# Two-layer attention in f32 on one core: a visit's two pair sums are folded into one before the product with ones

## The chip, the cores and the metric

The kernel runs on one core of a Trainium2 chip (trn2). The metric is device time in microseconds (us) of one execution, and the time before is the median of 3 runs. All arithmetic is in float32; a few operands are held as fp32r, a 32-bit format for products.

## The reference

`x` and `ctx` are [4, 1024, 512]. A softmax attention with 16 heads of 32 comes first, then a linear attention over the same context; both end in a layer norm.

```python
Q, K, V = heads(x @ Wq.T + bq), heads(ctx @ Wk.T + bk), heads(ctx @ Wv.T + bv)
att = softmax(Q @ K.T / sqrt(32))
x1 = layernorm((att @ V).merge() @ Wo.T + bo + x) * gamma0 + beta0
q_phi, k_phi = elu(x1), elu(ctx)
z = 1 / (q_phi @ k_phi.sum(axis=1) + 1e-6)
out = layernorm(x1 + (q_phi @ (k_phi.T @ ctx)) * z) * gamma1 + beta1
```

The softmax's denominator, the sum of the exponentials over the 1024 keys for each query and head, is what this change touches. It is the same sum after it, added in another order.

## The kernel before

The work of the first layer is cut into 64 units: 4 batches, 4 groups of four heads (QUAD), 4 chunks of 256 queries (CH). All five engines run the same counter `k` (a tick), from FIRST = -44 to LAST, and each writes its own instructions in the order of ticks; only semaphores hold them together. A unit takes 16 ticks. In tick `k`:

- TensorE (PE) does `pass1(k)` (L258): one product of 128 queries with 512 keys into one of three PSUM banks `score`, for the row maxima; VectorE (DVE) reduces it (`maximum`, L553). `pass1` waits until the maximum three uses back is taken.
- TensorE does `pass2(k-22)` (L282): the same scores turned, keys on partitions and queries along the row, into one of two banks `scoreT`; ScalarE (ACT) takes the exponential of a half step (`exponential`, L451) into `p_ring`, a ring of 8 key tiles of 4 x 256 columns.
- A planner, which is the same before and after, has spread "chains" over the ticks (`beside(k)`): the projections of K, V and Q, the output projection, the layer norms' tiles and the second layer.
- Once per unit, at tick 19 + 16u, `place_max(u)` (L267): the negated row maxima are turned by a product with the identity, and ScalarE copies them into rows 96 to 103 of `q_stack` (L441), from which `pass2` subtracts them. They come from VectorE, which at ticks 16, 17 and 18 (+16u) folds them (L563), rounds them (L570, a cast) and takes the rest of the rounding (L573, a tensor_tensor of `max_row` and `neg_max`). L573 is the instruction that `place_max` waits for (`max_split`).
- Every 8 ticks, at 35 + 8v, a visit `visit(v)`: 128 in all. TensorE first multiplies four key tiles of exponentials with V (L300) into `acc` columns 0 to 255, and then adds the denominators into `acc` columns 256 to 511 by products with a matrix of ones (L308). A product with ones sums over the 128 keys on the partitions, and its right-hand side is a sum of two key tiles that GpSimd (POOL) has added before (`add_pair`, L760: `pair_sum`, two slots, each written in two halves of 512 columns). Each f32 product of the program is two matrix instructions in the trace, so L300 has 32 of them per visit and L308 has 16, 8 for each of the two pairs.

Every other visit stands in the same tick as a `place_max` and right behind it: visit 2m at tick 35 + 16m behind `place_max(m+1)`. These ticks are called turns here; there are 63 of them and a first `place_max` without a visit.

GpSimd's `add_pair(pair, h)` stands at ticks 26 + 4·pair + h. Its first half waits until `divided` says that the products with ones have read the pair two before it, which lay in the same slot. So the first pair of visit v+1 waits for the first product of visit v. GpSimd also does the additions and scalings of the layer norms' tiles: L768 (bias), L773 and L776 (the root and the shift), L782 and L784, L789 and L791 (gamma and beta), and it adds features of the context (L803, L807).

VectorE's `normalise` (L582 to L597) divides `acc` by the denominators once a unit, after its second visit.

Of the kernel before, what the change touches and what calls it, by code (L numbers as in the profile page):

```python
# [7 lines left out]
ALU = mybir.AluOpType  # L8
# [4 lines left out]
def build(nc, x, xT, ctx, ctxT, WqT, bq, WkT, bk, WvT, bv, WoT, bo, gamma0, beta0, gamma1, beta1, out):  # L13
    B, S, D = x.shape
    P = nc.NUM_PARTITIONS
    DK = 32
    QUAD = P // DK
# [27 lines left out]
    FIRST = -44  # L45

# [4 lines left out]
    with ExitStack() as c:  # L51
# [6 lines left out]
        def sems(*names):  # L58
            return {n: c.enter_context(nc.semaphore(n)) for n in names}
# [66 lines left out]
                 "den_turned", "den_inverted", "den_back", "out_scaled", "f_phi", "ksum_kept", "y_summed",  # L126
# [3 lines left out]
        L = sems("cleared", "hot", "ident_made", "ones_made", "half_made", "paired", "totalled", "biased", "rooted0",  # L130
# [113 lines left out]
        def tensor_program():  # L244
# [42 lines left out]
            def visit(v):  # L287
# [16 lines left out]
                for s in range(VISIT // 2):  # L304
                    pair = VISIT // 2 * v + s
                    pe.wait_ge(L["paired"], 2 * (pair + 1))
                    for j in range(QUAD):
                        mm = pe.matmul(acc[j * DK:(j + 1) * DK, CH:2 * CH], ones[:, 0:DK],  # L308
                                       pair_sum[:, pair % 2, j * CH:(j + 1) * CH], start=False,
                                       stop=part == KT // VISIT - 1 and s == VISIT // 2 - 1,  # L310
                                       tile_position=(0, j * DK), skip_group_check=True)
                    mm.then_inc(T["divided"], 1)
# [231 lines left out]
        def vector_program():  # L544
# [31 lines left out]

            def normalise(unit, stage):
                if stage == 0:
                    dve.wait_ge(T["divided"], KT // 2 * (unit + 1))
# [132 lines left out]
            for k in range(FIRST, LAST):  # L712
# [32 lines left out]
                if k in phi_at:  # L745
                    make_phi(phi_at[k])
                unit, i = divmod(k - (VISIT_AT + 2 * VISIT + 1), UT)
# [4 lines left out]
        def gpsimd_program():  # L752
            pool = nc.gpsimd

            def add_pair(pair, h):
                n, cols = 2 * pair + 1, slice(h * HALF, (h + 1) * HALF)
                pool.wait_ge(A["exped"], 2 * n + h + 1)
                if h == 0 and pair >= 2:
                    pool.wait_ge(T["divided"], pair - 1)
                pool.tensor_tensor(pair_sum[:, pair % 2, cols], p_ring[:, (n - 1) % NP, cols], p_ring[:, n % NP, cols],  # L760
                                   ALU.add).then_inc(L["paired"], 1)
# [61 lines left out]
            for k in range(FIRST, LAST):  # L823
# [17 lines left out]
                if 0 <= pair < KT * UNITS // 2 and i < 2:  # L841
                    add_pair(pair, i)

# [170 lines left out]
```

## Time and profile before

| | before |
|---|---|
| median of 3 runs | 1755.48 us (1754.87 to 1761.07) |
| the profiled execution's own time | 1762.24 us |
| its span, first to last instruction | 1760.9 us |
| mean granted TensorE clock | 0.972 of 2.4 GHz |
| TensorE products busy | 1646.2 us (93%) |
| VectorE busy | 1070.9 us (61%) |
| GpSimd busy | 951.3 us (54%) |
| ScalarE busy | 880.9 us (50%) |

Busy times are sums over the whole span. Products of TensorE are pipelined and their ends are modelled, so how fast they follow each other is read from their starts. PEld is TensorE's weight load, which runs beside the products. In the timeline a row gives the start, the time to the last end of the merged instructions, the engine, the line, the operation with its operands and the count, and in brackets how long the engine had been idle and what ended that.

### The profile page before, as it was taken

The numbers are of one execution on the slowest core, as the hardware profiler recorded it, in microseconds if no ns is written. First come the engines' busy times: TensorE is split into PE (matmuls) and PEld (weight loads), VectorE is DVE, ScalarE is ACT, GpSimd is POOL, SyncE is SP. The second block draws the span as 40 slices with busy tenths as digits, with TensorE's granted clock in tenths as the row PEclk, the third lists the DMA queues.
The fourth block names the chain that finished last, engine by engine and source line by source line (L and its number), as shares of the span: only waits on it lengthen the run. The fifth ranks groups of instructions, "written<-read, shape, count | busy, mean of one in ns | idle before, by whom it ended". The sixth has DMA issues, their size and how long they took to land.

```text
span 1760.9 us, 32310 instructions
## 1 busy us (share of the span) xinstructions
PE 1646.2 (93%) x12176; PEld 1114.6 (63%) x12176; DVE 1070.9 (61%) x2216; ACT 880.9 (50%) x1617; POOL 951.3 (54%) x923
## 2 busy tenths in 40 slices
PE   6999999999999999999999999999999999999754
PEld 4667776676766666567666657657676767665321
DVE  2665557656666666567566756666666666666232
ACT  0355547555554554654554554665545554575321
POOL 0244535455655664455665655555566555566644
PEclk8999999999999999999999999999999999999877
DMA  8524162233315244141523234322322423200001
GB/s 252 159 63 132 55 204 78 73 99 103 108 40 138 79 130 162 55 115 39 144 79 110 74 103 146 110 85 91 112 72 91 122 74 102 97 24 13 25 24 36
DMA packets 149291, 168.05 MB, mean 95 GB/s; under 512 B 12816, under 2 KB 111120, under 8 KB 149136
## 3 DMA queue, kind: packets, MB, share of 16 engines
q1 hardware_dynamic: 149136, 165.99, 31.8%
q8 instruction: 97, 1.59, 0.4%
q14 instruction: 58, 0.48, 0.1%
HBM read 124.00 MB, written 41.94 MB: 94 GB/s over the span
## 4 chain that ended last, share of the span: by engine, by line
PE 81%; DVE 6%; POOL 4%; DMA 4%; issue 3%; ACT 2%; SPq 1%; DVEq 0%; ACTq 0%; POOLq 0%
PE acc L300 13%; PE score L258 13%; PE scoreT L282 12%; PE misc L375 6%; PE misc L329 6%; PE misc L367 6%; PE acc L308 6%; PE misc L339 6%; PE misc L351 5%; PE misc L319 4%; DVE maxes L553 2%; POOL pair_sum L760 1%; PE score L267 1%; DMA res_out<-ctx_nat 1%; DMA ctx_nat<-ctx_in 1%
## 5 line engine op out<-in xcount | busy, mean ns | idle before, releaser
L760 POOL TENSOR_TENSOR pair_sum<-p_ring 128x512 f32<-128x512 f32 x512 | 654.5, 1299 | 636.0 <-PE acc L308 568.5
L553 DVE TENSOR_REDUCE maxes<-score 128x1 f32<-128x512 f32 x1024 | 679.1, 678 | 441.6 <-PE score L258 440.5
L451 ACT ACTIVATE p_ring<-scoreT 128x512 f32<-128x512 f32 x1024 | 595.6, 594 | 616.8 <-PE scoreT L282 603.5
L258 PE MATMUL score<-k_stack,q_stack 96*128 96x512 f32 x1024 | 615.6, 603 | 8.7 <-DVE maxes L553 7.5
L282 PEld LDWEIGHTS scoreT<-q_stack,k_stack 104*128 104x128 f32 x2048 | 378.7, 191 | 187.8 <-ACT p_ring L451 114.4
L282 PE MATMUL scoreT<-q_stack,k_stack 104*128 104x256 f32 x2048 | 428.0, 291 | 16.3 <-ACT p_ring L451 14.8
L258 PEld LDWEIGHTS score<-k_stack,q_stack 96*128 96x128 f32 x1024 | 194.3, 190 | 170.4 <-issue 139.2
L300 PE MATMUL acc<-p_ring,v_sb 128*32 128x256 f32 x4096 | 279.4, 392 | 0.0
L300 PEld LDWEIGHTS acc<-p_ring,v_sb 128*32 128x32 f32 x4096 | 155.5, 112 | 81.6 <-ACT p_ring L451 22.2
L308 PE MATMUL acc<-pair_sum,ones 128*32 128x256 f32 x2048 | 159.3, 383 | 7.7 <-POOL pair_sum L760 7.7
L319 PE MATMUL misc<-xT_sb,wq 128*128 128x256 f32 x512 | 134.3, 386 | 10.1 <-DVE k_low L615 5.8
L329 PE MATMUL misc<-ctxT_sb,wk 128*128 128x512 f32 x256 | 133.2, 606 | 7.7 <-DMA ctxT_sb<-ctxT_in 6.9
L367 PE MATMUL misc<-kv_sb,ctx_nat 128*128 128x512 f32 x256 | 135.3, 623 | 4.5 <-issue 2.3
L339 PE MATMUL misc<-wv,ctxT_sb 128*128 128x128 f32 x1024 | 134.1, 275 | 0.0
L375 PE MATMUL misc<-ctx_nat,fphi_sb 128*128 128x512 f32 x256 | 132.1, 597 | 0.0
L351 PE MATMUL misc<-wo,outT 128*128 128x512 f32 x256 | 129.5, 597 | 0.0
L339 PEld LDWEIGHTS misc<-wv,ctxT_sb 128*128 128x128 f32 x1024 | 125.8, 192 | 0.6 <-DVE k_low L615 0.3
L308 PEld LDWEIGHTS acc<-pair_sum,ones 128*32 128x32 f32 x2048 | 87.2, 112 | 46.5 <-POOL pair_sum L760 10.0
L319 PEld LDWEIGHTS misc<-xT_sb,wq 128*128 128x128 f32 x512 | 90.2, 193 | 18.9 <-DVE k_low L615 6.0
L773 POOL TENSOR_TENSOR rstd<-var_eps,minus_half 128x1 f32<-128x1 f32 x64 | 36.5, 571 | 92.8 <-DVE var_eps L648 92.6
L441 ACT ACTIVATE q_stack<-score 8x1024 fp32r<-8x1024 f32 x64 | 65.0, 1016 | 41.5 <-PE score L267 41.0
L688 DVE SCALAR_TENSOR_TENSOR fphi_sb<-f_sb,ctx_nat 128x128 f32<-128x128 f32 x128 | 70.1, 547 | 22.6 <-ACT f_sb L506 11.0
(66 smaller groups left out, 1221.8 us busy)
## 6 DMA issues: line engine op xcount, KB each, us to landing
xT_sb<-xT_in SPq DMA_DIRECT2D x64, 512.0 KB, 4.1
k_stack<-k_dram SPq DMA_DIRECT2D x96, 256.0 KB, 4.4
q_stack<-q_dram SPq DMA_DIRECT2D x192, 128.0 KB, 2.5
ctxT_sb<-ctxT_in SPq DMA_DIRECT2D x8, 1024.0 KB, 7.3
k_dram<-k_high SPq DMA_DIRECT2D x32, 256.0 KB, 2.0
k_dram<-k_low SPq DMA_DIRECT2D x32, 256.0 KB, 2.6
q_dram<-q_high SPq DMA_DIRECT2D x64, 128.0 KB, 1.7
q_dram<-q_low SPq DMA_DIRECT2D x64, 128.0 KB, 1.9
```

Source lines behind the costliest of these rows:

```text
L258: pe.matmul(score[use % 3][:], q_stack[0:SPLIT, unit % NQ, j, t * P:(t + 1) * P], k_stack[0:SPLIT, unit // NC % 2 * QUAD + j, h * HALF:(h ...
L282: mm = pe.matmul(scoreT[k % 2][:, (j % 2) * CH:(j % 2 + 1) * CH], k_stack[0:ROWS, unit // NC % 2 * QUAD + j, kt * P:(kt + 1) * P], q_stack ...
L300: mm = pe.matmul(acc[j * DK:(j + 1) * DK, 0:CH], v_sb[:, group % 2, kt, j * DK:(j + 1) * DK], p_ring[:, n % NP, j * CH:(j + 1) * CH], star ...
L308: mm = pe.matmul(acc[j * DK:(j + 1) * DK, CH:2 * CH], ones[:, 0:DK], pair_sum[:, pair % 2, j * CH:(j + 1) * CH], start=False, stop=part == ...
L319: mm = pe.matmul(bank_of("Q", unit)[:, 0:CH], wq[:, t, :], xT_sb[:, unit % 2, t, :], start=t == 0, stop=t == G - 1)
L329: mm = pe.matmul(bank_of("K", i)[:], wk[:, t, :], ctxT_sb[:, h, t, :], start=t == 0, stop=t == G - 1)
L339: mm = pe.matmul(bank_of("V", i)[:, t * P:(t + 1) * P], ctxT_sb[:, h, f, t * P:(t + 1) * P], wv[:, f, :], start=f == 0, stop=f == G - 1)
L367: mm = pe.matmul(bank_of("A", tile)[:], phiT_sb[:, d * P:(d + 1) * P], kv_sb[:, d, :], start=d == 0, stop=d == G - 1)
L375: pe.matmul(bank_of("S", i)[:], fphi_sb[:, piece % NPHI, :], ctx_nat[:, t, :], start=t == 0, stop=t == KT - 1).then_inc(T["kv_piece"], 1)
L451: act.activation(p_ring[:, n % NP, h * HALF:(h + 1) * HALF], scoreT[k % 2][:], ACT.Exp, scale=SCALE).then_inc(A["exped"], 1)
L553: dve.reduce_max(maxes[:, unit % 2, t, j, h:h + 1], score[bank_use[k] % 3][:], AX.X).then_inc(V["maxed"], 1)
L760: pool.tensor_tensor(pair_sum[:, pair % 2, cols], p_ring[:, (n - 1) % NP, cols], p_ring[:, n % NP, cols], ALU.add).then_inc(L["paired"], 1)
```

## The change

The second pair's sum of a visit is added onto the first pair's before TensorE reads it: GpSimd adds columns 0 to 511 (`add_quad` in its program), VectorE columns 512 to 1023 (`add_quad` in its program). A visit then has one product with ones (8 matrix instructions) instead of two. The slots of `pair_sum` are dealt anew by `place_of_pair`: pairs 0, 1, 2, 3 lie in slots 0, 1, 1, 0, so the first pair of the next visit lies where the second pair of this one lay, and waits for both `add_quad` of this visit instead of for TensorE. The second pair of a visit waits for the visit before.

```diff
@@
+    def place_of_pair(pair):
+
+        return (pair // 2 + pair % 2) % 2
@@
-                for s in range(VISIT // 2):
-                    pair = VISIT // 2 * v + s
-                    pe.wait_ge(L["paired"], 2 * (pair + 1))
-                    for j in range(QUAD):
-                        mm = pe.matmul(acc[j * DK:(j + 1) * DK, CH:2 * CH], ones[:, 0:DK],
-                                       pair_sum[:, pair % 2, j * CH:(j + 1) * CH], start=False,
-                                       stop=part == KT // VISIT - 1 and s == VISIT // 2 - 1,
-                                       tile_position=(0, j * DK), skip_group_check=True)
-                    mm.then_inc(T["divided"], 1)
+                pe.wait_ge(L["quad_low"], v + 1)
+                pe.wait_ge(V["quad_high"], v + 1)
+                for j in range(QUAD):
+                    mm = pe.matmul(acc[j * DK:(j + 1) * DK, CH:2 * CH], ones[:, 0:DK],
+                                   pair_sum[:, place_of_pair(2 * v), j * CH:(j + 1) * CH], start=False,
+                                   stop=part == KT // VISIT - 1, tile_position=(0, j * DK), skip_group_check=True)
+                mm.then_inc(T["divided"], 1)
@@ vector_program
+            def add_quad(v):
+
+                first, second = (pair_sum[:, place_of_pair(2 * v + i), HALF:2 * HALF] for i in range(2))
+                dve.wait_ge(L["paired"], 4 * (v + 1))
+                dve.tensor_tensor(first, first, second, ALU.add).then_inc(V["quad_high"], 1)
+
             def normalise(unit, stage):
                 if stage == 0:
-                    dve.wait_ge(T["divided"], KT // 2 * (unit + 1))
+                    dve.wait_ge(T["divided"], KT // VISIT * (unit + 1))
@@
                 if k in phi_at:
                     make_phi(phi_at[k])
+                v, i = divmod(k - VISIT_AT + 2, 2 * VISIT)
+                if i == 0 and 0 <= v < VISITS:
+                    add_quad(v)
                 unit, i = divmod(k - (VISIT_AT + 2 * VISIT + 1), UT)
@@ gpsimd_program
                 pool.wait_ge(A["exped"], 2 * n + h + 1)
-                if h == 0 and pair >= 2:
-                    pool.wait_ge(T["divided"], pair - 1)
-                pool.tensor_tensor(pair_sum[:, pair % 2, cols], p_ring[:, (n - 1) % NP, cols], p_ring[:, n % NP, cols],
-                                   ALU.add).then_inc(L["paired"], 1)
+                if h == 0 and pair >= 2 and pair % 2:
+                    pool.wait_ge(T["divided"], pair // 2)
+                elif h == 0 and pair >= 2:
+                    pool.wait_ge(L["quad_low"], pair // 2)
+                    pool.wait_ge(V["quad_high"], pair // 2)
+                pool.tensor_tensor(pair_sum[:, place_of_pair(pair), cols], p_ring[:, (n - 1) % NP, cols],
+                                   p_ring[:, n % NP, cols], ALU.add).then_inc(L["paired"], 1)
+
+            def add_quad(v):
+
+                first, second = (pair_sum[:, place_of_pair(2 * v + i), 0:HALF] for i in range(2))
+                pool.wait_ge(L["paired"], 4 * v + 3)
+                pool.tensor_tensor(first, first, second, ALU.add).then_inc(L["quad_low"], 1)
@@
                     add_pair(pair, i)
+                if 0 <= pair < KT * UNITS // 2 and pair % 2 and i == 2:
+                    add_quad(pair // 2)
```

Three places of the engines' orders show it. The first is VectorE around a turn, in an early unit; the names in brackets are the semaphores waited for. Before, from the cast of the maxima (L570) to the next division of `acc` (L582):

```order
L570 CAST neg_max<-max_row 128x2x4 [waits max_turned,max_whole]
L553 TENSOR_REDUCE maxes<-score 128x1 [waits scored]
L573 TENSOR_TENSOR neg_max<-max_row,neg_max 128x2x4 [waits max_high]
L553 TENSOR_REDUCE maxes<-score 128x1 [waits scored] x10
L582 STREAM_TRANSPOSE den_rows<-acc 128x256 [waits out_scaled,divided]
```

And the same place now (the kernel's lines have moved, L570 is L572, L573 is L575, L553 is L555, L582 is L590):

```order
L572 CAST neg_max<-max_row 128x2x4 [waits max_turned,max_whole]
L583 TENSOR_TENSOR pair_sum<-pair_sum 128x512 [waits paired]
L555 TENSOR_REDUCE maxes<-score 128x1 [waits scored]
L575 TENSOR_TENSOR neg_max<-max_row,neg_max 128x2x4 [waits max_high]
L555 TENSOR_REDUCE maxes<-score 128x1 [waits scored] x7
L583 TENSOR_TENSOR pair_sum<-pair_sum 128x512 [waits paired]
L555 TENSOR_REDUCE maxes<-score 128x1 [waits scored] x3
L590 STREAM_TRANSPOSE den_rows<-acc 128x256 [waits out_scaled,divided]
```

One of a unit's two new additions (L583) stands between the cast and the subtraction of the maxima, the other seven maxima behind it.

The second place is GpSimd in the same early units, over one visit. Before:

```order
L760 TENSOR_TENSOR pair_sum<-p_ring 128x512 [waits divided,exped]
L760 TENSOR_TENSOR pair_sum<-p_ring 128x512 [waits exped]
L760 TENSOR_TENSOR pair_sum<-p_ring 128x512 [waits divided,exped]
L760 TENSOR_TENSOR pair_sum<-p_ring 128x512 [waits exped]
L760 TENSOR_TENSOR pair_sum<-p_ring 128x512 [waits divided,exped]
```

Now:

```order
L774 TENSOR_TENSOR pair_sum<-p_ring 128x512 [waits quad_high,quad_low,exped]
L774 TENSOR_TENSOR pair_sum<-p_ring 128x512 [waits exped]
L774 TENSOR_TENSOR pair_sum<-p_ring 128x512 [waits divided,exped]
L774 TENSOR_TENSOR pair_sum<-p_ring 128x512 [waits exped]
L781 TENSOR_TENSOR pair_sum<-pair_sum 128x512 [waits paired]
L774 TENSOR_TENSOR pair_sum<-p_ring 128x512 [waits quad_high,quad_low,exped]
```

A fifth addition (L781) follows a visit's four, and the next visit's first one waits for VectorE's half instead of for TensorE.

The third place is TensorE at a visit. Before:

```order
L282 MATMUL scoreT<-q_stack,k_stack 128x256 x2
L300 MATMUL acc<-p_ring,v_sb 32x256 x16
L308 MATMUL acc<-pair_sum,ones 32x256 x8
L258 MATMUL score<-k_stack,q_stack 128x512
L282 MATMUL scoreT<-q_stack,k_stack 128x256 x2
```

Now:

```order
L286 MATMUL scoreT<-q_stack,k_stack 128x256 x2
L304 MATMUL acc<-p_ring,v_sb 32x256 x16
L311 MATMUL acc<-pair_sum,ones 32x256 x4
L262 MATMUL score<-k_stack,q_stack 128x512
L286 MATMUL scoreT<-q_stack,k_stack 128x256 x2
```

Four products with ones (8 matrix instructions in the trace) are gone; nothing else has moved.

## Rows read from the trace of the kernel before

**Rows 1.** The page: busy time, share and instructions; then the granted clock.

```profile
PE 1646.2 (93%) x12176; PEld 1114.6 (63%) x12176; DVE 1070.9 (61%) x2216; ACT 880.9 (50%) x1617; POOL 951.3 (54%) x923
...
PEclk8999999999999999999999999999999999999877
```

**Rows 2.** Groups by line: busy us, mean ns of one | idle before, releaser.

```profile
L760 POOL TENSOR_TENSOR pair_sum<-p_ring 128x512 f32<-128x512 f32 x512 | 654.5, 1299 | 636.0 <-PE acc L308 568.5
...
L300 PE MATMUL acc<-p_ring,v_sb 128*32 128x256 f32 x4096 | 279.4, 392 | 0.0
...
L308 PE MATMUL acc<-pair_sum,ones 128*32 128x256 f32 x2048 | 159.3, 383 | 7.7 <-POOL pair_sum L760 7.7
```

**Rows 3.** Waits: us in total, times, longest us.

```profile
POOL pair_sum L760 <- PE acc L308: 568.5, 126, 9.2
...
PEld score L267 <- DVE neg_max L573: 32.1, 38, 1.6
...
PEld acc L308 <- POOL pair_sum L760: 10.0, 6, 6.4
...
PE score L267 <- DVE neg_max L573: 15.8, 20, 1.4
...
PE score L258 <- DVE maxes L553: 7.5, 20, 0.9
```

**Rows 4.** Timeline of TensorE, visit 3, which is no turn.

```profile
109.66 1.93 PE L300 MATMUL acc<-p_ring,v_sb 128*32 128x256 f32 x32
...
111.42 1.05 PE L308 MATMUL acc<-pair_sum,ones 128*32 128x256 f32 x16
...
112.39 0.50 PE L258 MATMUL score<-k_stack,q_stack 96*128 96x512 f32 x1
```

**Rows 5.** Timeline, VectorE and TensorE at the turn of unit 2.

```profile
100.86 0.16 DVE L570 CAST neg_max<-max_row 128x8 fp32r<-128x8 f32 x1
100.93 0.68 DVE L553 TENSOR_REDUCE maxes<-score 128x1 f32<-128x512 f32 x1
...
101.53 0.15 DVE L573 TENSOR_TENSOR neg_max<-max_row,neg_max 128x8 fp32r<-128x8 f32 x1
...
101.74 0.28 PE L267 MATMUL score<-ident,neg_max 128*8 128x128 f32 x1 [0.69 <-DVE neg_max L573]
...
105.41 4.88 DVE L553 TENSOR_REDUCE maxes<-score 128x1 f32<-128x512 f32 x8 [3.12 <-PE score L258]
```

**Rows 6.** Timeline of GpSimd, the four additions ahead of that turn.

```profile
93.94 4.99 POOL L760 TENSOR_TENSOR pair_sum<-p_ring 128x512 f32<-128x512 f32 x4 [5.64 <-PE acc L308]
```

**Rows 7.** Timeline at the turn of unit 19, with GpSimd busy.

```profile
498.61 0.34 DVE L570 CAST neg_max<-max_row 128x8 fp32r<-128x8 f32 x1
498.87 0.68 DVE L553 TENSOR_REDUCE maxes<-score 128x1 f32<-128x512 f32 x1
498.89 1.26 POOL L782 TENSOR_TENSOR ctx_nat<-ctx_nat,gamma_row 128x512 f32<-128x512 f32 x1
499.47 0.70 DVE L573 TENSOR_TENSOR neg_max<-max_row,neg_max 128x8 fp32r<-128x8 f32 x1
...
500.22 0.28 PE L267 MATMUL score<-ident,neg_max 128*8 128x128 f32 x1 [1.39 <-DVE neg_max L573]
```

**Rows 8.** One line's instructions: duration ns, min/median/max.

```profile
L573 DVE TENSOR_TENSOR neg_max<-max_row,neg_max x64: 149/156/1190, 60.2 to 1621.5; 128x8 fp32r<-128x8 f32 x64
...
L656 DVE SCALAR_TENSOR_TENSOR ctx_nat<-ctx_nat x32: 682/1124/1741, 393.0 to 1743.5; 128x512 f32<-128x512 f32 x32
```

**Rows 9.** Timeline at the turns of units 12 and 13: subtraction done, turn begun.

```profile
325.38 0.15 DVE L573 TENSOR_TENSOR neg_max<-max_row,neg_max 128x8 fp32r<-128x8 f32 x1
...
325.97 0.28 PE L267 MATMUL score<-ident,neg_max 128*8 128x128 f32 x1
...
352.01 0.16 DVE L573 TENSOR_TENSOR neg_max<-max_row,neg_max 128x8 fp32r<-128x8 f32 x1
...
353.78 0.28 PE L267 MATMUL score<-ident,neg_max 128*8 128x128 f32 x1
```

**Rows 10.** The chain that ended last, its piece around the last visits.

```profile
1636.90 2.51 POOL pair_sum L760 x2
1639.42 1.23 POOL ctx_nat L789
...
1661.08 1.23 POOL pair_sum L760
1662.35 1.08 PE acc L308 x8
```

More of the change, by code:

```diff
@@ L125, in build @@
         V = sems("hot_rows", "k_low_kept", "q_low_kept", "v_kept", "maxed", "max_whole", "max_high", "max_split",
-                 "den_turned", "den_inverted", "den_back", "out_scaled", "f_phi", "ksum_kept", "y_summed",
+                 "quad_high", "den_turned", "den_inverted", "den_back", "out_scaled", "f_phi", "ksum_kept", "y_summed",
                  "counted0", "aggregated0", "var_added0", "phi_made", "dotted", "z_added", "z_inverted",
                  "y_attended", "counted1", "aggregated1", "var_added1", "bias_spread", "bias_folded")
-        L = sems("cleared", "hot", "ident_made", "ones_made", "half_made", "paired", "totalled", "biased", "rooted0",
+        L = sems("cleared", "hot", "ident_made", "ones_made", "half_made", "paired", "quad_low", "totalled", "biased", "rooted0",
                  "shifted0", "scaled0", "x1", "rooted1", "shifted1", "scaled1", "result")
```

## The prediction

> **What bounds the kernel now.** I read the page first. TensorE's products are busy 93% of the span, no other engine more than 61%, and the granted clock is at its upper level, 2.4 GHz, in nearly every slice until the last [rows 1]. The waits come next: of the many thousand products very few wait for anybody. VectorE's maxima hold `pass1` up for 7.5 us in all, and the largest wait inside the steady part is `place_max` for the subtraction L573: 20 times TensorE itself stood idle, 15.8 us in all, and 38 times the weight load did [rows 3]. So whatever shortens TensorE's own work shortens the run, and whatever comes late at `place_max` lengthens it. GpSimd waits 568.5 us for TensorE's products with ones [rows 3]; it has time, but it is held up.
>
> **What goes away.** 128 visits lose 8 of 16 instructions of L308. Two prices can be read. By the group's busy time half of 159.3 us goes, 79.6 us [rows 2]. But these are modelled ends that overlap. By the starts, the 32 instructions of L300 hand over to L308 after 111.42 - 109.66 = 1.76 us, 55 ns each; and L308's 16 hand over to `pass1` after 112.39 - 111.42 = 0.97 us [rows 4]. 16 x 55 ns are 0.88 us, the rest (0.1 us) is the run-out at the end, which stays. I take 8 x 55 ns = 0.44 us per visit, x 128 = **-56 us**, and keep 79.6 for the range.
>
> **What is added on GpSimd.** 128 additions of 128x512, 1.30 us each [rows 2], 166 us. GpSimd is free for that: 951 us of 1761 busy, and it loses most of the 568.5 us in which it waits for TensorE, because a visit's first pair no longer waits for the products with ones. Cost on the path: 0, as long as `quad_low` comes before TensorE ends the V products of the visit. At the turn of unit 2 GpSimd's four pair additions end at 93.94 + 4.99 = 98.93 [rows 6], the fifth would end at 100.2, and TensorE asks for it 1.76 us after the turn's start at 101.74 [rows 4, 5], at 103.5. Where GpSimd is late by a layer norm's two additions (2.6 us) that margin is just used up; its earlier start of the first pair gives these back.
>
> **What is added on VectorE.** 128 additions of 128x512 with both inputs in SBUF. The trace has no such addition. The nearest is L656, as wide and with two inputs in SBUF, 682 ns at the shortest [rows 8]; eight maxima in a row, 680 ns each by their own rows, take 4.88 us, 0.61 us from start to start [rows 5]. So an addition puts 0.61 us into VectorE's row and its result is there after 0.69. The Trainium skill, VectorE: DVE Perf Modes, section The TRN2 errata, gives (N+151)/0.96 ns for such an addition, 691 ns, which agrees with L656; its section The DRAIN you can't avoid says that the next instruction does not start before the pipeline is empty. By that rule it would cost the full 0.69, some 4 us more over the run; the maxima show 0.61 and I stay with them.
>
> Half of these, 64, stand behind nothing urgent: the addition before visits 1, 3, 5 and so on (no turns) is followed by two maxima, and TensorE then spends 2.7 us on the visit, in which VectorE sits idle (3.12 us at a turn [rows 5]). They cost 0, and if that cover were gone, 0.6 us each, 38 us.
>
> The other 63 are the point. They stand between the cast L570 and the maximum ahead of L573, and L573 releases TensorE at the turn. First the 0.61 us. Then a second thing. When VectorE's half is done, GpSimd is released for the next visit's first pair, whose exponentials are long there, and starts at once. L573 reads two operands in SBUF, and such instructions do not run while GpSimd adds: alone it takes 156 ns [rows 8]; at unit 19 GpSimd began an addition at 498.89, L573 began at 499.47 and ended at 500.17, 20 ns behind GpSimd's end at 500.15 [rows 7]. TensorE started 0.05 us later, and its wait was 1.39 instead of the 0.69 us of a quiet turn [rows 5, 7].
>
> So, from the cast's end: before, the maximum starts at 0, L573 at 0.60, is done at 0.75, TensorE starts at 0.80 [rows 5]. After: the addition starts at 0, the maximum at 0.61, the addition is done at 0.69, GpSimd runs from 0.74 to 2.01, L573 could start at 1.21 but ends at 2.04, TensorE starts at 2.09. A turn is **1.3 us later**, more than what its own visit and the next one save together (0.88).
>
> Whether TensorE feels it depends on the slack of the turn. In 20 turns it was already idle (15.8 us [rows 3]): full 1.3 each, 26 us. In the other 18 of the 38 where only the load queue waited, the slack is like unit 12's: L573 done at 325.53, turn begun at 325.97, 0.4 us of slack [rows 9], so 0.9 each, 16 us. In the remaining 26 (25 turns and the first `place_max`) the slack is longer, up to unit 13's 1.6 us [rows 9]; between 0.6 and 0 each I take 0.3, 8 us. Together **+50 us**. Bounds: without the lock-out by GpSimd 20 x 0.6 + 18 x 0.2 = 16 us; with no slack anywhere 63 x 1.3 = 82 us.
>
> **The tail.** Around the last two visits the chain runs over GpSimd and DMA [rows 10]. The first pair of visit 126 no longer waits for visit 125 (2.5 us at 1636.90), and two fifth additions come in (2 x 1.3). I take 0, within 3 us either way.
>
> **Sum.** 1762.24 - 56 + 50 = 1756.2 us against the profiled execution's own time, 6 us less. That execution lies 6.8 us above the median of 1755.48, so against the median the forecast is **1750 us**: the products saved are handed back at the turns.
>
> **Rival A, the turns cost little.** L573 slips in before GpSimd starts, or TensorE has more slack there than I read: then the turns cost 16 us, and the time is 1755.5 - 56 + 16 = 1716. For it: GpSimd could be at another instruction, or the second half of that pair's exponentials could hold it. Against it: L573's 0.70 in [rows 7], and its longest of 1190 ns [rows 8]. The Trainium skill, SBUF — State Buffer, section SBUF: two separate sides, calls the port pair an exclusive lock that the first comer keeps for its whole instruction; by that the rival would need GpSimd idle, and the trace agrees. 0.13.
>
> **Rival B, the products with ones are dearer than their pitch.** The saving is the 79.6 us of the busy time, and the time is 1755.5 - 79.6 + 50 = 1726. Against it stands the regular pitch in [rows 4]. 0.10.
>
> **Rival C, VectorE waits for GpSimd at the turns: slower.** VectorE's addition needs GpSimd's pair, and in the moment the pair is ready GpSimd begins its own fifth addition and shuts VectorE's out for 1.28 us. It decides where the pair ends less than 1.3 us before the cast is done. At unit 2 the distance is 101.02 - 98.93 = 2.1 us [rows 5, 6], a margin of 0.8; at unit 19 the cast itself was held until 498.95 by an addition [rows 7], so there the margin is gone. If it is gone at the 38 turns with little slack, at 0 to 1.28 us and 0.64 on the mean, that adds 24 us: 1774. Against it: GpSimd starts the pairs earlier than before. 0.17.
>
> **That it doesn't do what it says** is excluded by the order of the instructions: 4 products with ones per visit instead of 8, five GpSimd additions instead of four.
>
> **How the numbers follow.** A difference of 0.5%, 8.8 us, is about what a measurement of this kernel can tell from none: faster means below 1746.7, slower above 1764.3. My forecast's own range is 1738 to 1764 (turns between 38 and 64 us), chance 0.55, of which 0.20 lies below 1746.7. Rivals A and B, 0.23, are all faster. Rival C, 0.17, is slower but for 0.02; small things in its direction (a visit that waits for `quad_low`) or mine make 0.05 more within 0.5%. Faster 0.43, same 0.42, slower 0.15. The range takes in nearly all of A and C: 1718 to 1776.
>
> **What would show it.** The wait of `place_max` for VectorE's subtraction grows from 15.8 us to some 60 us, in 50 turns or more instead of 20; the subtraction's median goes from 156 ns to about 0.8 us, ending with a GpSimd addition; L308's successor has half its count and 0.53 us from its start to the next `pass1`; GpSimd's wait for TensorE, 568.5 us, nearly vanishes; `pass1`'s wait for the maxima stays below 20 us. The forecast is wrong if the subtraction stays at 156 ns (rival A), if the visit shrinks by 0.6 us or more (B), or if VectorE's new addition itself has a mean far above 0.7 us at the turns (C).

## The result, and the profile after

The changed kernel is slower: 1783.3 us at the median of 4 runs (1782.0 to 1784.8) against 1757.0 of the kernel before beside it, ratio 1.0147 (95% interval 1.0125 to 1.0169). The forecast was 1750 us, range 1718 to 1776: the time lies outside it. The profiled execution took 1781.96 us, 19.7 more than the one of before (1762.24).

The page of the changed kernel, busy times and granted clock, beside [rows 1]:

```profile
PE 1610.7 (90%) x11152; PEld 1100.2 (62%) x11152; DVE 1212.2 (68%) x2344; ACT 883.0 (50%) x1617; POOL 1134.8 (64%) x1051
...
PEclk9999999999999999999999999999999999898877
```

TensorE has 1024 matrix instructions less and is busy 35.5 us less, and the run is longer all the same. The list of waits of the changed kernel (us in total, times, longest), which answers to [rows 3]:

```profile
POOL pair_sum L774 <- DVE pair_sum L583: 146.9, 66, 5.3
...
PE score L271 <- DVE neg_max L575: 66.5, 53, 2.7
...
PEld acc L311 <- POOL pair_sum L781: 25.3, 8, 10.9
...
PE acc L311 <- DVE pair_sum L583: 11.2, 7, 3.7
...
PE score L262 <- DVE maxes L555: 7.3, 21, 0.9
```

`place_max` (now L271) waits 66.5 us for the subtraction instead of 15.8, in 53 turns instead of 20. GpSimd's wait for TensorE is gone. The subtraction itself, by its own line (ns, min/median/max), beside the 156 ns of [rows 8]:

```profile
L575 DVE TENSOR_TENSOR neg_max<-max_row,neg_max x64: 153/934/1220, 58.4 to 1637.2; 128x8 fp32r<-128x8 f32 x64
```

And one turn in the timeline, that of unit 2, the same as in [rows 5]:

```profile
99.49 0.16 DVE L572 CAST neg_max<-max_row 128x8 fp32r<-128x8 f32 x1
99.56 0.69 DVE L583 TENSOR_TENSOR pair_sum<-pair_sum 128x512 f32<-128x512 f32 x1
100.16 0.69 DVE L555 TENSOR_REDUCE maxes<-score 128x1 f32<-128x512 f32 x1
100.42 2.50 POOL L774 TENSOR_TENSOR pair_sum<-p_ring 128x512 f32<-128x512 f32 x2 [2.45 <-ACT p_ring L453]
100.76 0.94 DVE L575 TENSOR_TENSOR neg_max<-max_row,neg_max 128x8 fp32r<-128x8 f32 x1
...
101.76 0.39 PE L271 MATMUL score<-ident,neg_max 128*8 128x128 f32 x2 [2.06 <-DVE neg_max L575]
```

The addition takes 0.60 us from its start to the next, GpSimd is released and starts at 100.42 (0.17 us behind the addition's end at 100.25; I had put it at 0.05), and the subtraction ends at 101.70, when GpSimd's first half (1.28 us) does. From the cast's end at 99.65 to TensorE's start are 2.11 us; before they were 101.74 - 101.02 = 0.72. A turn without slack waits 2.06 us instead of 0.69.

The visit is shorter as forecast: at visit 3, which is no turn, the products with ones and what follows are

```profile
110.99 0.61 PE L311 MATMUL acc<-pair_sum,ones 128*32 128x256 f32 x8
111.53 0.50 PE L262 MATMUL score<-k_stack,q_stack 96*128 96x512 f32 x1
```

0.54 us apart, where [rows 4] have 0.97. Summed over 127 visits, from the start of the products with ones to the next start behind them, it is 95.0 us instead of 150.6: 55.6 us saved.

So the two terms of my sum are right to a microsecond each (-55.6 against -56, and the 50.7 us by which the waits of `place_max` grew against +50), and what makes the time wrong is something else. The granted clock in stretches of 100 us shows most of it (columns: stretch, length, busy us and instructions of PE, PEld, DVE, ACT, POOL, then the granted clock, DMA share, GB/s). Before:

```profile
100.00:200.00 100.00, 95.69 (x852) 70.91 (x852) 60.50 (x122) 52.18 (x89) 49.02 (x40) 1.00 0.33 95
...
1100.00:1200.00 100.00, 97.52 (x698) 62.02 (x698) 64.75 (x130) 61.80 (x142) 54.47 (x64) 1.00 0.34 103
```

After:

```profile
100.00:200.00 100.00, 90.80 (x752) 66.58 (x753) 68.84 (x122) 49.12 (x85) 58.34 (x47) 0.97 0.31 92
...
1100.00:1200.00 100.00, 93.75 (x608) 58.77 (x599) 73.89 (x133) 59.45 (x137) 64.03 (x71) 0.95 0.29 88
```

A stretch of 100 us with a granted clock of 0.95 has spent 10 us at 1.2 GHz and the rest at 2.4 GHz. Over the steady part, from 60 us to visit 122, the records of the granted clock add up to 20.5 us at 1.2 GHz before and 61.4 us after; over the whole span the mean fell from 0.972 to 0.959, and it is 0.956 to 0.959 in all four runs. What the lower clock costs is seen at a turn at 1121 us:

```profile
1121.84 0.38 PE L271 MATMUL score<-ident,neg_max 128*8 128x128 f32 x1 [2.06 <-DVE neg_max L575]
1121.95 0.65 PE L304 MATMUL acc<-p_ring,v_sb 128*32 128x256 f32 x3
...
1125.34 0.67 PE L311 MATMUL acc<-pair_sum,ones 128*32 128x256 f32 x3
```

TensorE stands idle 2.06 us, and the visit behind it runs its products with V in 3.4 us (1121.95 to 1125.34) instead of 1.75. The falls lie at such waits: of the 15 in the steady part of the changed kernel 9 begin within 1 us of the end of a wait of 2.0 to 2.7 us at a turn. Such a wait does not always bring a fall: 17 turns wait longer than 2 us.

The balance of the 19.7 us, read from the starts of all visits. Up to visit 122, products with ones -51.6, waits at the turns +48.8 (the last 1.7 of the 50.5 lie behind it), the time from a visit's first product with V to its first with ones +19.7 (14 of it in visits at 1.2 GHz, 6 in visits 45, 77 and 109, which wait for VectorE's half), and everything else -3.4; together visit 122 starts 13.5 us later. Over the whole run the waits of `pass2` for ScalarE alone are 9.6 us shorter (5.2 instead of 14.8). Visit 45 shows how a half comes late: GpSimd finishes the second pair only at 620.66, and then its own fifth addition holds VectorE's, which takes 1.74 us instead of the median 0.68.

```profile
619.38 1.28 POOL L774 TENSOR_TENSOR pair_sum<-p_ring 128x512 f32<-128x512 f32 x1
620.63 1.26 POOL L781 TENSOR_TENSOR pair_sum<-pair_sum 128x512 f32<-128x512 f32 x1
620.70 1.74 DVE L583 TENSOR_TENSOR pair_sum<-pair_sum 128x512 f32<-128x512 f32 x1 [2.32 <-POOL pair_sum L774]
```

Behind visit 122 come 6.3 us more. They are TensorE's waits at the products with ones of visits 126 and 127: 14.1 us (3.7 and 10.4) instead of 7.7, and behind the last of them both kernels take 98 us more. In visit 127 GpSimd finishes the second pair at 1677.8 and starts its fifth addition only at 1680.63, because two instructions of a layer norm (L802 and L804, gamma and beta) stand between them in its order:

```profile
1676.52 1.26 POOL L774 TENSOR_TENSOR pair_sum<-p_ring 128x512 f32<-128x512 f32 x1
1677.73 1.26 POOL L802 TENSOR_TENSOR ctx_nat<-ctx_nat,gamma_row 128x512 f32<-128x512 f32 x1
1679.08 1.59 POOL L804 TENSOR_TENSOR ctx_nat<-ctx_nat,beta_row 128x512 f32<-128x512 f32 x1
1680.63 1.26 POOL L781 TENSOR_TENSOR pair_sum<-pair_sum 128x512 f32<-128x512 f32 x1
```

### The profile page after: what moved, and what is told of

The parts are those of the page before. It is cut to its first block, busy times and chain, and to the rows that moved or that the text cites. A ratio compares the mean times of both kernels' runs of the same rounds, so it can differ in the third digit from the quotient of the medians.

```text
span 1780.6 us, 30646 instructions
## 1 busy us (share of the span) xinstructions
PE 1610.7 (90%) x11152; PEld 1100.2 (62%) x11152; DVE 1212.2 (68%) x2344; ACT 883.0 (50%) x1617; POOL 1134.8 (64%) x1051
## 4 chain that ended last, share of the span: by engine, by line
PE 71%; DVE 15%; POOL 5%; issue 4%; DMA 3%; ACT 2%; SPq 0%; DVEq 0%; ACTq 0%; POOLq 0%
PE acc L304 14%; PE score L262 11%; PE scoreT L286 10%; PE misc L369 6%; PE misc L377 6%; PE misc L341 5%; PE misc L331 5%; DVE maxes L555 5%; PE misc L321 4%; PE acc L311 4%; PE misc L353 4%; DVE neg_max L575 2%; DVE pair_sum L583 2%; POOL pair_sum L774 1%; PE score L271 1%
## 5 line engine op out<-in xcount | busy, mean ns | idle before, releaser
L555 DVE TENSOR_REDUCE maxes<-score 128x1 f32<-128x512 f32 x1024 | 680.9, 678 | 320.7 <-PE score L262 320.1
L304 PE MATMUL acc<-p_ring,v_sb 128*32 128x256 f32 x4096 | 289.8, 405 | 0.0
L304 PEld LDWEIGHTS acc<-p_ring,v_sb 128*32 128x32 f32 x4096 | 171.2, 116 | 74.3 <-ACT p_ring L453 22.6
L781 POOL TENSOR_TENSOR pair_sum<-pair_sum 128x512 f32<-128x512 f32 x128 | 166.5, 1301 | 0.0
L793 POOL TENSOR_TENSOR rstd<-var_eps,minus_half 128x1 f32<-128x1 f32 x64 | 41.9, 655 | 143.9 <-DVE var_eps L656 143.9
L583 DVE TENSOR_TENSOR pair_sum<-pair_sum 128x512 f32<-128x512 f32 x128 | 109.9, 859 | 31.5 <-POOL pair_sum L774 31.5
L311 PE MATMUL acc<-pair_sum,ones 128*32 128x256 f32 x1024 | 104.9, 393 | 21.6 <-DVE pair_sum L583 11.2
L271 PE MATMUL score<-ident,neg_max 128*8 128x128 f32 x256 | 43.3, 298 | 66.5 <-DVE neg_max L575 66.5
```

Of the source, the lines that this page charges most:

```text
L304: mm = pe.matmul(acc[j * DK:(j + 1) * DK, 0:CH], v_sb[:, group % 2, kt, j * DK:(j + 1) * DK], p_ring[:, n % NP, j * CH:(j + 1) * CH], star ...
L555: dve.reduce_max(maxes[:, unit % 2, t, j, h:h + 1], score[bank_use[k] % 3][:], AX.X).then_inc(V["maxed"], 1)
```

## The experiments

The runs e1 to e4 tell the parts apart, e5 to e8 test the cause of the lower clock and cheap remedies, e9 to e11 move `place_max` itself. Ratios are to runs of the kernel before on the same chip beside them, whose median was 1762.2 us for e1 to e4, 1759.3 for e5 to e8 and 1758.8 for e9 to e11. The columns: TensorE's own wait in `place_max`; time at 1.2 GHz between 60 us and visit 122; start of visit 122.

| kernel | ratio (95% interval) | wait at turns, us | 1.2 GHz, us | visit 122 at, us |
|---|---|---|---|---|
| before | 1 | 16 | 20 | 1599 |
| changed | 1.0147 (1.0125 to 1.0169) | 66 | 61 | 1613 |
| e1_tick34 | 0.9798 (0.9778 to 0.9818) | 20 | 27 | 1559 |
| e2_pool_held | 0.9967 (0.9950 to 0.9983) | 42 | 58 | 1587 |
| e3_no_quads | 0.9776 (0.9756 to 0.9795) | 31 | 44 | 1564 |
| e4_two_products | 1.0438 (1.0418 to 1.0457) | 66 | 72 | 1669 |
| e5_turns_late | 0.9792 (0.9765 to 0.9818) | 20 | 31 | 1557 |
| e6_stall_alone | 1.0251 (1.0228 to 1.0274) | 44 | 61 | 1640 |
| e7_addition_alone | 1.0182 (1.0159 to 1.0205) | 36 | 51 | 1628 |
| e8_last_two | 0.9793 (0.9766 to 0.9819) | 20 | 34 | 1555 |
| e9_place_inside | 0.9801 (0.9777 to 0.9825) | 7 | 34 | 1558 |
| e10_late_and_inside | 0.9755 (0.9732 to 0.9778) | 1 | 17 | 1548 |
| e11_before_inside | 0.9939 (0.9918 to 0.9961) | 0 | 17 | 1587 |

### e1_tick34: VectorE's addition behind the subtraction

```diff
-                v, i = divmod(k - VISIT_AT + 2, 2 * VISIT)
+                v, i = divmod(k - VISIT_AT + 1, 2 * VISIT)
                 if i == 0 and 0 <= v < VISITS:
                     add_quad(v)
```

> The changed kernel with VectorE's new addition one tick later in its order, behind the subtraction of the maxima (tick 34 + 8v instead of 33 + 8v); all else as changed. The turn theory (the addition and the GpSimd addition that it releases stand before the subtraction that place_max waits for, and the 10 more windows of half clock in the changed kernel are a consequence of those stalls): the subtraction's median goes back to about 0.16 us, place_max waits under 18 us instead of 66.5, the half-clock windows in the steady part go back to 7 or so, and the time is about 1757 - 56 + 5 (tail) + 5 (visits that wait for a half) = 1711 us. The load theory (the clock falls because VectorE and GpSimd do more at the same time as TensorE, wherever the addition stands): the stalls go but the extra half clock stays, some 18 us: 1729 us. The late-halves rival (the visit's own waits for the two additions cost as much as the turns did): 1750 us or more, with VectorE's addition waited for at the products with ones.

Measured: ratio 0.9798, 1721 us on the scale of 1757. The subtraction's line and the waits at the turns in this kernel:

```profile
L575 DVE TENSOR_TENSOR neg_max<-max_row,neg_max x64: 149/156/1190, 59.1 to 1580.7; 128x8 fp32r<-128x8 f32 x64
...
  PE score L271: 19.0, 20
```

One place in VectorE's order is worth 3.5% of the time. The change as it was made loses 1.5%, the same change with the addition 0.7 us later wins 2.0%. The turn theory holds (the waits are 19.0 us, a little over the 18 forecast), the late-halves rival falls, and so does the load theory: the load is the same and the time at 1.2 GHz is down from 61 to 27 us. Of the 10 us over the forecast of 1711 some 7 are the visits' own waits for the two halves: 11.8 us up to visit 122, where I had put 5 (over the whole run 16.7 us in 15 visits for VectorE's half and 8.6 for GpSimd's).

### e2_pool_held: GpSimd released only behind the subtraction

```diff
                     pool.wait_ge(V["quad_high"], pair // 2)
+                    if pair % 4 == 2 and pair < 228:
+                        pool.wait_ge(V["max_split"], (pair - 2) // 4 + 2)
```

> The changed kernel, but GpSimd holds the next visit's first pair addition at 57 of the 63 turns until the subtraction of the maxima is done, so only VectorE's own addition stays ahead of the subtraction. If the turn's 1.3 us is made of 0.6 (VectorE's addition) and 0.7 (the lock-out by GpSimd's pair addition): the subtraction's median falls from 0.93 to 0.16 us, place_max's wait falls from 66.5 to about 30 us, and the time from 1783 to about 1747 or, with fewer half-clock windows, 1740. If the lock-out is not what holds the subtraction: the median stays near 0.9 and the time within 5 us of 1783.

Measured: ratio 0.9967; the waits are 41.4 us in 36 turns, the median 157 ns:

```profile
L575 DVE TENSOR_TENSOR neg_max<-max_row,neg_max x64: 147/157/1037, 59.8 to 1611.6; 128x8 fp32r<-128x8 f32 x64
```

The lock-out is what held the subtraction. Of the 50.7 us more at the turns 25 belong to GpSimd's released addition, and 22 to VectorE's own (from here to e1_tick34). The waits that are left are somewhat more than forecast, 41 against 30 us; six of the turns weren't held. The span is 26 us shorter than the changed kernel's. On the scale of 1757 the time is 1751, where I had forecast 1747, or 1740 with a recovered clock: the clock did not recover, with 58 us at 1.2 GHz against 61. So 24 us less of stalls gave 26 us back here, and the time at 1.2 GHz does not go in proportion to the stalls.

### e3_no_quads: the product alone

Neither addition is made; the second pair of each visit is left out of the denominators.

```diff
-                pe.wait_ge(L["quad_low"], v + 1)
-                pe.wait_ge(V["quad_high"], v + 1)
+                pe.wait_ge(L["paired"], 4 * (v + 1))
...
                 elif h == 0 and pair >= 2:
-                    pool.wait_ge(L["quad_low"], pair // 2)
-                    pool.wait_ge(V["quad_high"], pair // 2)
+                    pool.wait_ge(L["paired"], 2 * pair)
```

> The changed kernel without both new additions: the product with ones reads the first pair's sum alone, and the second pair is left out of the denominators. It still waits for both pairs, and GpSimd's pairs are in the new slots. It measures what the product that is gone is worth by itself. By the pitch of the instructions (0.44 us a visit): 1757 - 56 = 1701 us, 1695 to 1708 with the few waits at turns that are left. By the modelled busy time (79.6 us): 1678. If the clock fell because TensorE issues fewer products (and not because of stalls), the extra half-clock windows are here too and the time is near 1718.

Measured: 0.9776, 1718 on the scale of 1757, not 1701. The products with ones are shorter by the full 53 us, and 15 us of it are lost at the turns (31 instead of 16 us) with 44 us at 1.2 GHz. The cause is in the slots: a visit's first pair no longer waits for TensorE, so GpSimd adds close to the turn, with no new addition anywhere. Here it is the cast ahead of the subtraction that is held: its median is 725 ns instead of 160, the subtraction's stays at 157. At the turn of unit 2 GpSimd adds from 96.16 to 98.65, and the cast ends 0.03 us behind it:

```profile
96.16 2.49 POOL L769 TENSOR_TENSOR pair_sum<-p_ring 128x512 f32<-128x512 f32 x2 [1.37 <-ACT p_ring L452]
...
97.57 1.11 DVE L571 CAST neg_max<-max_row 128x8 fp32r<-128x8 f32 x1
```

The forecast for this run named 1718 for a clock that falls with the number of products. The number came true, and the mechanism is another: e6_stall_alone has all the products and the lower clock, e10_late_and_inside has the fewer products and 17 us at 1.2 GHz. So the number can't stand for that theory.

### e4_two_products: the additions alone

TensorE issues the product with ones twice from the same sum, so the denominators come out doubled.

```diff
-                for j in range(QUAD):
-                    mm = pe.matmul(acc[j * DK:(j + 1) * DK, CH:2 * CH], ones[:, 0:DK],
...
+                for s in range(2):
+                    for j in range(QUAD):
+                        mm = pe.matmul(acc[j * DK:(j + 1) * DK, CH:2 * CH], ones[:, 0:DK],
...
```

> The changed kernel with the product with ones issued twice from the same sum (denominators doubled): the additions and their waits as changed, TensorE's work as before. It measures the additions' cost alone. If gain and cost add up, 1783 + 56 = 1839 us, place_max's wait again 60 to 70 us, and again 15 or more half-clock windows in the steady part. If the shorter visit was part of the cause of the stalls or of the lower clock (VectorE and GpSimd have less time to catch up), the time stays below 1825 and place_max waits for less.

Measured: 1.0438; the profiled span is 1837.7 us, 57.1 more than the changed kernel's. The two ratios put it at 51 us, uncertain by some 5, since the changed kernel and this one were measured beside different runs of the kernel before. `place_max` waits 66.0 us, as in the changed kernel. Gain and cost add up: the shorter visit had no part in the stalls.

### e5_turns_late and e8_last_two: two refinements

```diff
-                v, i = divmod(k - VISIT_AT + 2, 2 * VISIT)
-                if i == 0 and 0 <= v < VISITS:
-                    add_quad(v)
+                for late in range(2):
+                    v, i = divmod(k - VISIT_AT + 2 - late, 2 * VISIT)
+                    if i == 0 and 0 <= v < VISITS and (v % 2 == 0) == bool(late):
+                        add_quad(v)
```

> The changed kernel with VectorE's new addition behind the subtraction of the maxima at the turns (tick 34, as in the run e1_tick34, ratio 0.980), but left at tick 33 + 8v at the other visits, where nothing waits for the subtraction. In e1_tick34 8 of those other visits waited 0.45 us for it, and visits 45, 51, 77, 83 and 109 about 2 us. If the later place caused the short waits, they go (3.6 us) and perhaps two of the long ones: ratio 0.976 to 0.979. If placement at the other visits does not matter, 0.980.

Measured: 0.9792 against 0.9798, within the intervals. The short waits for VectorE's half went (15 waits of 16.7 us became 7 of 13.5), the long ones stayed.

In e8_last_two VectorE also makes GpSimd's half of visits 126 and 127:

```diff
+                if v >= VISITS - 2:
+                    lows = [pair_sum[:, place_of_pair(2 * v + i), 0:HALF] for i in range(2)]
+                    dve.tensor_tensor(lows[0], lows[0], lows[1], ALU.add).then_inc(V["quad_last"], 1)
```

> The run e5_turns_late with GpSimd's half of the last two visits given to VectorE too. In the changed kernel GpSimd's fifth additions stand in the chain of the last visits (1663.0 and 1680.7 us), and the stretch from visit 122 to the end took 167.9 instead of 161.6 us. If the fifth additions lengthen it, it becomes 2 to 3 us shorter than in e5_turns_late; if the tail's length is set by the layer norms' loads and stores alone, it stays within 1 us.

Measured: the stretch from visit 122 to the end is 163.3 us against 164.0, the ratio 0.9793. Within 1 us, but this edit moves the work and does not take it away: in visits 126 and 127 TensorE now waits 10.9 us for VectorE where it waited 12.4. So it does not clear the additions. e3_no_quads, which has neither, takes 159.9 us for this stretch with 8.3 us of such waits, against 163.3 to 169.1 us in the eight kernels with both additions and 161.6 in the kernel before.

### e6_stall_alone: a stall and no work

```diff
                 pe.wait_ge(V["max_split"], unit + 1)
+                pe.wait_ge(V["maxed"], min(PLACE + UT * unit + 1, HALVES))
```

> The kernel before with one added wait and no added work: at each turn place_max also waits until VectorE has taken the maximum of its own tick. TensorE then stands still some 0.3 to 0.6 us longer at most turns, and no engine does anything more. If stalls at the turns are what brings the half-clock windows: place_max's waits grow from 16 to 40 to 50 us, the windows between 60 us and visit 122 from 20 us to 45 or more, and the time grows by the stalls plus some 10 us, to a ratio of 1.02 to 1.03. If the additional work of VectorE and GpSimd brings them: the windows stay at 20 us or so and the ratio is 1.015 to 1.02, by the stalls alone.

Measured: 1.0251. Every engine has the kernel before's work. TensorE stands 27.7 us longer at the turns (44 against 16), and visit 122 starts 41.0 us later. Three stretches of this kernel, for the clock:

```profile
100.00:200.00 100.00, 93.44 (x819) 68.31 (x821) 56.63 (x113) 49.37 (x84) 44.90 (x36) 0.97 0.32 93
400.00:500.00 100.00, 95.05 (x702) 66.88 (x700) 63.54 (x136) 50.12 (x85) 55.68 (x51) 0.98 0.31 93
1100.00:1200.00 100.00, 96.46 (x709) 63.47 (x708) 63.18 (x129) 56.42 (x122) 49.36 (x55) 0.97 0.32 101
```

The time at 1.2 GHz rises from 20 to 61 us, as in the changed kernel, and all four runs have a mean clock of 0.960 or 0.961 where the seven runs of before beside them have 0.967 to 0.975. So stalls at the turns cost more than their own length here: 13 us on top of 28. The visits show where: from first product with V to first with ones they take 14.7 us more in all.

### e7_addition_alone: VectorE's addition, waited for by nobody

The kernel before, with one addition more into a new buffer `scratch`.

```diff
+                v, i = divmod(k - VISIT_AT + 2, 2 * VISIT)
+                if i == 0 and 0 <= v < VISITS:
+                    dve.wait_ge(M["rows"], 5 * 16)
+                    if v > 0:
+                        dve.wait_ge(V["added"], v)
+                    dve.tensor_tensor(scratch[:], gamma0_row[:], beta0_row[:], ALU.add).then_inc(V["added"], 1)
```

> The kernel before with a 128x512 addition of two constant rows into a buffer that nobody reads, at the place in VectorE's order where the change has its own; nothing waits for it and GpSimd is not released by it. The turn theory says 0.6 us of the 1.3 us belong to this addition: place_max's waits 16 us to about 35 us (20 turns by 0.6, 18 by 0.2, plus lock-outs by chance), the subtraction's median stays 0.16, ratio 1.01 to 1.02, half-clock windows somewhat above 20 us. If the whole cost of a turn came from the addition and none from the released GpSimd work, place_max's waits would be near 66 us and the ratio 1.04.

Measured: 1.0182, waits 35.6 us in 32 turns. The addition's own part is 20 us of stalls, as the split of 0.6 and 0.7 says, and 9 more came with them (visit 122 starts 29 us later, with 51 us at 1.2 GHz).

### e9, e10, e11: the turned maxima inside the visit

TensorE does `place_max` between the visit's products with V and its product with ones. In the changed kernel (e9_place_inside), with the additions of e5_turns_late (e10_late_and_inside) and in the kernel before (e11_before_inside):

```diff
                 mm.then_inc(T["weighted"], 1)
+                if v % 2 == 0 and v // 2 + 1 < UNITS:
+                    place_max(v // 2 + 1)
...
-                if i == 0 and 0 <= unit < UNITS:
+                if i == 0 and unit == 0:
                     place_max(unit)
```

> The changed kernel with VectorE's and GpSimd's orders untouched; only TensorE does place_max between the visit's products with V and its product with ones instead of ahead of the visit. The 1.3 us by which the subtraction is late then lies beside 1.75 us of products with V. If the turn was all that made the changed kernel slow: place_max's waits fall from 66.5 us to a few, the half-clock windows before visit 122 from 61 us to 20 or 30, and the ratio to before becomes 0.970 to 0.980. If ScalarE's copy of the turned maxima (1.0 us, now 1.8 us later) becomes the next wait, part comes back as waits of pass2 for ScalarE: 0.98 to 0.99.

> Both remedies: VectorE's addition behind the subtraction at the turns (e5_turns_late, ratio 0.979) and place_max between the products with V and with ones. The 19.6 us of waits left at the turns should go and some half clock with them: ratio 0.963 to 0.970. If the subtraction is no longer urgent, this kernel and e9_place_inside differ by less than 0.003, since it no longer matters where VectorE's addition stands.

> The kernel before with place_max between the visit's products with V and with ones, nothing else. It had 16 us of waits there, and some half clock: 1757 - 16 - 5 = 1736, ratio 0.988. Against e9_place_inside it gives what the change is worth where no turn is in its way: 56 us of products less some 6 us of waits at visits and in the tail, that is a ratio between the two of 0.970 to 0.975. If ScalarE's later copy costs TensorE a wait, the ratio is 0.995 or above.

Measured: 0.9801, 0.9755 and 0.9939. e9 leaves VectorE and GpSimd as in the changed kernel, the subtraction's median is still 0.95 us, and the kernel goes from 1.5% slower to 2.0% faster, since the 1.75 us of products with V now lie over it. TensorE's waits for ScalarE in `pass2` rose from 5.2 us in the changed kernel to 17.4. Waits of TensorE in e10_late_and_inside:

```profile
PE acc L313 <- DVE pair_sum L585: 17.4, 10, 3.8
PE scoreT L286 <- ACT p_ring L455: 15.4, 18, 2.3
PE acc L313 <- POOL pair_sum L784: 11.9, 4, 8.6
```

`place_max`'s wait is down to 1.4 us and the time at 1.2 GHz to 17 us. But 10 us of new waits for ScalarE came in (15.4 us; in e5_turns_late 5.0): its copy of the turned maxima now comes later, before the first `pass2` that needs it. The waits at the products with ones are 7 us longer too (29.3 us against 22.2). These two fit the distance from the forecast of 0.963 to 0.970; no run takes them apart. e9 and e10 differ by 0.005, more than the 0.003 I allowed: e9 still has waits of 7 us at its turns, and twice the time at 1.2 GHz. e10_late_and_inside beats both kernels, 1713.5 us against 1758.8.

e11 came out at 0.9939 where I had forecast 0.988: the 16 us of waits at the turns are gone, and TensorE's waits for ScalarE in `pass2` rose from 14.8 to 23.2 us. Against e11, the same order without the change, the change is worth 0.985 in e9 and 0.981 in e10, the latter some 33 us of the 56 that it takes from TensorE. I had expected 0.970 to 0.975.

## Why the prediction was wrong

- **What goes away**, -56 us: right. 55.6 us by the starts of the visits, and 57.1 between the profiled spans of the changed kernel and e4_two_products. Rival B (79.6 us by busy times) is refuted: ends of overlapping products are no price, starts are.
- **GpSimd's additions cost 0 in the steady part**: nearly right; it is waited for in 8 visits by the weight loads, 1.2 to 2.2 us each in six of them, and the long ones (4.1 and 10.9 us) lie in the tail.
- **VectorE's addition, 0.61 us into its row**: right, 0.60 in the timeline. In the prediction I took the Trainium skill, VectorE: DVE Perf Modes, section The DRAIN you can't avoid, to ask for the full 0.69. That was half of what it states: the same paragraph says that a next operation that is not held starts earlier. The row agrees with that, the next maximum starts 0.60 us behind the addition's start.
- **The turn, 1.3 us and +50 us in all**: right, 1.37 us at a turn without slack and +50.7 us. The 20 turns that waited before gave 24 of it (forecast 26), the others 26.5 (forecast 24). The split of 0.6 for the addition and 0.7 for GpSimd's lock-out fits e2, e7 and e1. A slip on the way did no harm: from the cast's end to TensorE's start the rows give 0.72 us and not 0.80, because I counted from the start of the next instruction, before and after alike.
- **The additions before the other visits cost 0**: off by the 6 us of visits 45, 77 and 109, where GpSimd's layer-norm additions delay the visit's second pair, VectorE's addition waits for it, and GpSimd's fifth addition then holds it up.
- **The sum** is the step that failed. It left the granted clock at its level of [rows 1] and took a stall of TensorE to cost its own length. The stalls at the turns brought TensorE down to 1.2 GHz for three times as long, 61 us instead of 20 up to visit 122, which cost some 14 us in the visits' products with V; e6_stall_alone shows the same with stalls alone, 13 us on top of 28. In e2_pool_held the stalls fell by 24 us and the time at 1.2 GHz by only 3, so no price per microsecond of stall can be read from these runs. With the 6 us of the late halves, 6 us in the tail and some 3 us gained elsewhere this makes up the 19.7 us of the profiled executions.
- **The tail**, taken as 0 within 3 us: off by 6.3 us. TensorE waits 14.1 us for the additions of the last two visits instead of 7.7, and without the additions (e3_no_quads) the stretch is no longer than before.
- **The conversion to the median** was wrong too: I took off 6.8 us because one profiled execution of before lay that far above the median. Later medians of the kernel before were 1757 to 1762 us, so this was scatter of the runs, and the changed kernel's profiled execution lay 1.3 us below its median. Some 7 of the 33 us between 1750 and 1783 are this, the other 26 are the distance between the -6 us forecast for the profiled execution and its +19.7.
- **Rival A** fell with the subtraction's median of 934 ns.
- **Rival C** had the right sign and almost the right time (1774) and the wrong mechanism: VectorE's addition took more than 0.8 us at only 6 of the 63 turns, and its median is 682 ns. It took as long at 22 other visits, and at 45, 77 and 109 it was held as C describes, by GpSimd's fifth addition. The rival that should have stood there was my own mechanism with its stalls priced by what a stall costs, not by its length. The fall of the granted clock in the tail of [rows 1] was there to ask the question.

## What to carry to other kernels

Before a piece of work is laid onto an engine with time to spare, look which of its instructions releases the critical engine next, and put the work behind that one: here one place in VectorE's order separates 1.5% slower from 2.0% faster, with the same work. Work on GpSimd that is released by the new instruction counts as part of it, when the instructions that come next on the releasing engine are ones that GpSimd's additions hold up, as the subtraction and the cast here. And where the critical engine is TensorE, stalls can cost more than their length: 41 us for 28 in e6_stall_alone.

## What the runs showed of the hardware that was not expected

- Stalls of TensorE of 1 to 3 us, once every 25 us, bring the granted clock down now and then, with TensorE busy 91 to 98 us of the 100 us around them: 16, 20, 31, 36, 42, 44 and 66 us of stalls at turns go with 20, 27 to 34, 44, 51, 58, 61 and 61 to 72 us at 1.2 GHz in ten of the kernels above. e9 has 34 us at 1.2 GHz with 7 us of waits at turns, and waits elsewhere.
- A subtraction of 128x8 on VectorE that takes 156 ns alone takes 934 ns at the median when GpSimd's additions of two SBUF operands run beside it. It ends 21 to 28 ns behind a GpSimd instruction whenever it takes more than 250 ns (59 of 64 times in the changed kernel), and so gets in between two that follow each other without a gap. A cast of 128x8, which reads one operand, is held in the same way: 725 ns at the median in e3_no_quads, 160 in the kernel before.
